# Six clips and the decay and bonus columns of the first recurrence, made on POOL instead of DVE

## The reference, cut to what matters

```python
tf = sigmoid(sum(time_emb, -1))[:, None, None]
decay = exp(-exp(w))[None, :] * (0.5 + 0.5 * tf[:, :, 0])
ek  = exp(minimum(k, 30.0));  ekv = ek * v
# forward and backward scans over time:  a = a*decay + ekv_t ;  b = b*decay + ek_t
euk = exp(minimum(u + k, 30.0))
num = nf + nb - ekv + euk * v
den = df + db - ek + euk
base = sigmoid(r) * (num / maximum(den, 1e-08))
out = base * (0.8 + 0.2 * tf)
```

## Time and profile before

| | before |
|---|---|
| median of 3 runs | 438.07 us |
| the profiled execution | 438.29 us |
| its span, first to last instruction | 436.6 us |
| mean granted TensorE clock | 0.975 |
| busy: PE, DVE, POOL, ACT | 389.6, 327.8, 248.0, 232.9 us |

### The profile page before, as it was taken

One profiled execution on the slowest core, in us unless ns is written; L12 is line 12 of the kernel. 1 busy time (PEld: TensorE's weight loads), 2 busy tenths in 40 slices (PEclk: granted clock), 3 DMA queues, 4 the chain that ended last, 5 costly groups with the idle time before them and its releaser, 6 DMA issues.

```text
span 436.6 us, 6831 instructions
## 1 busy us (share of the span) xinstructions
PE 389.6 (89%) x2025; PEld 244.8 (56%) x2025; DVE 327.8 (75%) x620; ACT 232.9 (53%) x462; POOL 248.0 (57%) x347
## 2 busy tenths in 40 slices
PE   7898999999899999975895899999999999886895
PEld 7676788655455555643685445455445545563463
DVE  5998798999999999979887456654855452068993
ACT  5724594466676766757785423232322323259792
POOL 5475008489678998424840655785687366124641
PEclk9999999999999999999995699999999999999998
DMA  6910003455465644329311277926975710330011
GB/s 205 411 64 0 2 1 148 179 189 171 170 222 198 210 166 162 127 81 368 132 50 48 79 261 244 389 92 233 328 233 192 279 39 14 96 128 0 24 38 36
DMA packets 27347, 65.57 MB, mean 150 GB/s; under 512 B 3360, under 2 KB 7840, under 8 KB 26672
## 3 DMA queue, kind: packets, MB, share of 16 engines
q1 hardware_dynamic: 24320, 58.93, 38.9%
q0 software_dynamic: 1904, 5.18, 3.8%
q10 hardware_dynamic: 1088, 1.05, 0.7%
HBM read 102.83 MB, written 4.78 MB: 247 GB/s over the span
## 4 chain that ended last, share of the span: by engine, by line
PE 52%; DVE 29%; issue 8%; DMA 4%; ACT 4%; POOL 1%; SPq 1%; DVEq 0%; POOLq 0%; ACTq 0%
PE bank L2055 14%; PE bank L2089 8%; PE bank L1822 7%; DVE hx L1341 4%; DVE fw L1130 4%; DVE bw L1133 3%; PE bank L1667 3%; PE bank L1668 3%; PE bank L1669 3%; DVE fw L1138 2%; DMA dn<-in_dn 2%; PE bank L2066 2%; PE bank L1919 2%; DVE xp L1399 2%; PE bank L1744 2%
## 5 line engine op out<-in xcount | busy, mean ns | idle before, releaser
L2055 PE MATMUL bank<-gu,xbT 128*64 128x512 f32 (+1 forms) x320 | 71.3, 583 | 1.2 <-ACT xbT L964 0.9
L1822 PE MATMUL bank<-hx,w2raw 128*128 128x512 f32 x128 | 67.3, 607 | 4.6 <-DVE hx L1341 3.8
L852 ACT ACTIVATE rl<-bank 128x512 f32<-128x512 f32 x64 | 38.1, 595 | 38.3 <-PE bank L1669 37.5
L1562 DVE TENSOR_TENSOR hm<-bank,sl 128x512 f32<-128x512 f32 (+1 forms) x20 | 13.5, 675 | 48.8 <-issue 31.8
L1667 PE MATMUL bank<-xlhi,w1hi 128*128 128x512 f32 x64 | 49.3, 771 | 0.0
L2055 PEld LDWEIGHTS bank<-gu,xbT 128*64 128x64 f32 x320 | 25.9, 137 | 33.8 <-issue 28.8
L1341 DVE TENSOR_TENSOR hx<-bank,cwb 128x512 f32<-128x512 f32 x64 | 42.0, 659 | 3.1 <-ACT bank L856 3.0
L1138 DVE RECIPROCAL fw<-fw 128x256 f32<-128x256 f32 x23 | 39.8, 1730 | 0.0
L2089 PE MATMUL bank<-dn,hT 128*64 128x256 f32 x304 | 37.0, 384 | 2.7 <-ACT hT L976 0.3
L856 ACT ACTIVATE bank<-rl 128x512 f32<-128x512 f32 x64 | 38.1, 597 | 0.0
L634 POOL DMA_INDIRECT y_rows<-yb,dest_i x19 | 21.4, 1126 | 22.8 <-ACT yb L983 21.6
(11 more groups left out here) (312 smaller groups left out, 913.5 us busy)
## 6 DMA issues: line engine op xcount, KB each, us to landing
gu<-in_gu SPq DMA_DIRECT2D x86, 512.0 KB
dn<-in_dn SPq DMA_DIRECT2D x43, 512.0 KB
cwb<-cw_rows SPq DMA_DIRECT2D x32, 512.0 KB, 4.1
traw<-in_t SPq DMA_DIRECT2D x3, 1024.0 KB, 7.4
w1raw<-in_w SPq DMA_DIRECT2D x8, 256.0 KB, 4.7
w2raw<-in_w SPq DMA_DIRECT2D x8, 256.0 KB, 4.3
kT<-in_kt SPq DMA_DIRECT2D x4, 256.0 KB, 5.5
x<-in_x SPq DMA_DIRECT2D x2, 512.0 KB, 7.2
```

Source lines behind the costliest of these rows:

```text
L852: act.activation(rl[:, u % 3, :], bank[u % 4][:], ACT.Relu).then_inc(sem("r_ready"), 1)
L1822: pe.matmul(bank[4 + s][:], w2raw[:, e // 4 % 2, e % 4, :], hx[:, 0, u % 4, :], start=(e == 0), stop=(e == E0 - 1), skip_group_check=True) ...
L2055: ins = pe.matmul(bank[2 * (b % 2) + up][part(g), inner(b)], xbT[:, b % 2, k, part(g)], rhs, start=(k == 0), stop=(k == KC - 1))
```

## The change

Clips of batches 1 to 3 (six instructions) and the columns move from DVE's program to POOL's. On POOL a clip has a second operation, max with 0.0, which changes no value since an exponential is not negative. The `ubk` copy becomes four instructions, one per layer. DVE's first decay product signals `decay_ready`, which POOL waits for ahead of the columns. The semaphore `te_sum` counts the columns' instructions; DVE's `clip_key(0)` and `clip_bonus(0)` stay.

```diff
+            def clip_key(b):
+                pool.wait_ge(sem("ek_raw"), b + 1)
+                pool.tensor_scalar(ekk[:, 2 * b:2 * b + 2, 1, :], ekk[:, 2 * b:2 * b + 2, 1, :], E30, 0.0, ALU.min, ALU.max
+                                   ).then_inc(sem("ek_ready"), 1)
+            def clip_bonus(b):
+                pool.wait_ge(sem("eu_raw"), 2 * b + 2)
+                pool.tensor_scalar(GT[:, 1, 2 * b:2 * b + 2, :], GT[:, 1, 2 * b:2 * b + 2, :], E30, 0.0, ALU.min, ALU.max
+                                   ).then_inc(sem("euk_ready"), 1)
+            def side_columns():
+                per_b = tfb[:].rearrange("p i (o b q) -> p i o b q", o=1, q=1)
+                lbk = [P, 4, B, KC]
+                pool.wait_ge(sem("decay_ready"), 1)
+                pool.tensor_tensor(dec[:], wl[:].rearrange("p l (o k) -> p l o k", o=1).to_broadcast(lbk),
+                                   per_b[:, 2, :, :, :].to_broadcast(lbk), ALU.mult).then_inc(sem("te_sum"), 1)
+                for l in range(4):
+                    pool.tensor_scalar(ubk[:, l, :, :], ul[:, l:l + 1, :].to_broadcast([P, B, KC]), 1.0, 0.0, ALU.mult, ALU.add
+                                       ).then_inc(sem("te_sum"), 1)
+                pool.tensor_scalar(tfb[:, 3, :], tfb[:, 0, :], 0.2, 0.8, ALU.mult, ALU.add).then_inc(sem("te_sum"), 1)
+                pool.tensor_scalar(tfb[:, 1, :], tfb[:, 0, :], -0.2, -0.8, ALU.mult, ALU.add).then_inc(sem("te_sum"), 1)
...
             side_value(0)
+            clip_key(1)
             first_value(0)
             first_value(1)
             side_value(1)
+            clip_bonus(1)
+            side_columns()
+            clip_key(2)
             first_value(2)
+            clip_bonus(2)
             side_value(2)
+            clip_key(3)
             first_value(3)
+            clip_bonus(3)
             split_side(0)
             side_value(3)
             first_value(4)
...
-            pool.wait_ge(sem("te_sum"), 2)
+            pool.wait_ge(sem("te_sum"), 8)
...
-            def side_columns():
-                dve.tensor_tensor(dec[:], wl[:].rearrange("p l (o k) -> p l o k", o=1).to_broadcast(lbk),
-                                  per_b[:, 2, :, :, :].to_broadcast(lbk), ALU.mult)
-                dve.tensor_copy(ubk[:], ul[:].rearrange("p l (o k) -> p l o k", o=1).to_broadcast(lbk)).then_inc(sem("te_sum"), 1)
-                dve.tensor_scalar(tfb[:, 3, :], tfb[:, 0, :], 0.2, 0.8, ALU.mult, ALU.add)
-                chain(dve.tensor_scalar(tfb[:, 1, :], tfb[:, 0, :], -0.2, -0.8, ALU.mult, ALU.add))
...
-            between = {(0, 1): [lambda: clip_bonus(0), side_columns], (0, 3): [lambda: clips(1)],
-                       (1, 3): [lambda: clips(2)], (2, 3): [lambda: clips(3)],
+            between = {(0, 1): [lambda: clip_bonus(0)],
                        (5, 3): [lambda: make_cond(0, 0), lambda: make_cond(0, 1)],
```

More of the change, by code:

```diff
@@ L1082, in clip_bonus @@
                                   ).then_inc(sem("euk_ready"), 1)
-            def clips(b):
-                clip_key(b)
-                clip_bonus(b)
             dve.wait_ge(sem("wl_ready"), 3)
@@ L1091, in _ @@
             chain(dve.tensor_scalar(tfb[:, 2, :], tfb[:, 0, :], 0.5, 0.5, ALU.mult, ALU.add))
-            lbk, per_b = [P, 4, B, KC], tfb[:].rearrange("p i (o b q) -> p i o b q", o=1, q=1)
+            per_b = tfb[:].rearrange("p i (o b q) -> p i o b q", o=1, q=1)
             decf = dec[:].rearrange("p l b k -> p (l b k)")
[L1094 to L1097, removed]
-            def side_columns():
-                dve.tensor_tensor(dec[:], wl[:].rearrange("p l (o k) -> p l o k", o=1).to_broadcast(lbk),
-                                  per_b[:, 2, :, :, :].to_broadcast(lbk), ALU.mult)
-                dve.tensor_copy(ubk[:], ul[:].rearrange("p l (o k) -> p l o k", o=1).to_broadcast(lbk)).then_inc(sem("te_sum"), 1)
-                dve.tensor_scalar(tfb[:, 3, :], tfb[:, 0, :], 0.2, 0.8, ALU.mult, ALU.add)
-                chain(dve.tensor_scalar(tfb[:, 1, :], tfb[:, 0, :], -0.2, -0.8, ALU.mult, ALU.add))
+            dve.tensor_tensor(bank[6][:, 0:NBLK].rearrange("p (b k) -> p b k", k=KC),
+                              wl[:, 0:1, :].to_broadcast([P, B, KC]),
+                              per_b[:, 2, 0, :, :].to_broadcast([P, B, KC]), ALU.mult).then_inc(sem("decay_ready"), 1)
+            dve.wait_ge(sem("decay_ready"), 1)
             def col(ap, i):
```

## The result

The changed kernel takes 433.33 us (median of 7 runs, 432.89 to 434.69), the kernel before 436.6 (7 runs): ratio 0.9923, 95% interval 0.9904 to 0.9942. The same kernel again, in a later comparison: 434.13 against 436.64, ratio 0.9941 (0.9919 to 0.9962). I had forecast 439.4, slightly slower. The chance for what happened, rival 1, was 0.19.

The account below looks back on a forecast made before the run. DVE was taken as saturated up to its gain at 39.90 us; 2.98 us off DVE, less 0.25, plus 4.06 of waits for POOL gave +1.3 us: 439.4 us against a median of 438.07, range 438.1 to 440.3.

Parts of the forecast that it names:

- rival 1: POOL's clips cost 0.62 us, or anything under 1.33; POOL keeps up, DVE saves 2.7 us: 435.4 us; chance 0.19.
- What bounds the stage: From 6.24 to 40.3 us DVE is saturated, while POOL has 12.1 us free.
- the hand-over one to one: A microsecond DVE saves or loses ahead of its gain at 39.90 us shifts everything behind by as much.
- What DVE gives up: Columns and clips of batches 1 to 3, blocks 0 to 2: 2.98 us off DVE, 2.7 us net.
- The 0.25 for PE's warm-up: At DVE's first reciprocal, about 0.25 us of saving lost waiting for PE's first denominator, held by a warm-up assumed fixed.
- the columns' 0.99: DVE's column instructions, from 8.24 us to the next scan at 9.23: 0.99 us saved by moving them.
- the price of a clip: Called c: one min-max clip of 512 elements on POOL, estimated 2.0 us, six clips 12.0 us; bounds 0.62 and 2.29.
- the 4.06 us of waits for POOL: DVE's newton_step of blocks 3 and 4 waits for POOL's first_value, 1.89 and 2.17 us.
- The walk along POOL: POOL's queue added up in order from start-to-start lengths; first_value(4) ends at 31.1 us, leaving DVE 1.3 us late.
- Rival 3: PE idles about 2 us twice at blocks 3 and 4, its clock falls: 443 us; chance 0.04.
- Rival 2: Clips cost 2.29 us or more, or POOL's reads are slowed; between clip_bonus(3) and first_value(4): 441.2 us; chance 0.18.
- Rival 4: PE's adds, not DVE, set the stage's pace, so the change doesn't shorten it: 438 us; chance 0.04.

Follow-up runs that it names:

- The kernel with the prices: The changed kernel plus eleven tensor_scalar instructions in POOL's idle time, to time operation pairs; min-max took 0.61 us, add-min 1.93 us; no median given.
- The kernel with add-min: The changed kernel with POOL's clips written as add 0.0 then min, not min then max: 438.41 us, ratio 1.0039 to the kernel before.

## Why the prediction was wrong, step by step

- What bounds the stage, DVE's saturation and the hand-over one to one: right. The gain came 2.65 us earlier and layer 0's matmuls behind it 2.6.
- What DVE gives up, 2.7 us net: the number is right, partly by luck. Measured at the gain are 2.65, or 2.78 counted from DVE's first clip. Up to the first reciprocal 1.69 us were saved (12.83 to 11.27, and DVE had started 0.13 later), where 1.64 had been added up; the clips of batches 2 and 3 gave 1.09 together and not 1.34. The 0.25 for PE's warm-up did not show: its 36 matmuls took 6.04 us in the profile after and 7.09 before, so PE was ready earlier, and the two errors cancel. That was a length I took for fixed, and in another profile the term is there. The kernel with the prices holds the whole change, its warm-up was long, DVE waited 0.25 us, and its gain came at 37.56:

```profile
3.02 7.18 PE L1743 MATMUL bank<-ident 128*128 128x128 f32 x36 [3.02 <-POOL ident L474]
...
11.54 1.76 DVE L1220 RECIPROCAL fw<-bank 128x256 f32<-128x256 f32 x1 [0.25 <-PE bank L1805]
```

- Part of the columns' 0.99 was no work of theirs: one instruction lasted 0.70 instead of 0.15 beside POOL. Its like falls on another instruction when only one part is moved, so each part alone was worth less.
- **The step that failed is the price of a clip: 2.0 us estimated, 0.62 measured.** I saw that the pair of operations sets the price, and then put min-max into the slow class because L503 "has a minimum in it". The rows had two classes and none of them min-max; a minimum in another pair says nothing of this one. The lower bound, L557, was the truth. With it went the 4.06 us of waits for POOL: DVE had none, and the shift is -2.65 where +1.3 stood.
- The forecast of 439.4 was also counted from 438.07, the median of three runs; seven runs give 436.6. Of the 6.1 us between forecast and measurement 4.0 are the shift, 1.5 are this, and some 0.6 are left. Rival 1's 435.4 lies too high for the same reason, while its mechanism is the one that was found.
- The walk along POOL: right. Given the price of a clip it forecast the end within 0.2 us at c = 2.0 and 1.57 and DVE's waits within 0.3 at c = 2.0. Rival 1 used it too, to say that POOL keeps up.
- The Trainium skill's rule that 1-input work is near line rate on GpSimd (GPSIMD Engine Reference, section When to use GPSIMD) puts add, multiply and max in one row and tells no pairs apart. It holds within half as much again for min-max and multiply-add (0.61 to 0.62 us against an estimated 0.43 from the page) and fails by a factor of 3.5 for min alone and of four to five for add-min, add-add and max-multiply.
- Rival 3, PE's clock during the stage: no fall after the change, but there PE had no long waits either. The kernel with add-min is the test: PE stood idle 2.41 and 2.29 us for POOL, and the granted clock was 1.00 in every window from 15 to 41.4 us. Rival 2 had c of 2.29 or more; max-multiply came nearest, 2.27 from start to start. Rival 4, PE and not DVE sets the pace: out, since the gain came earlier by what DVE gave up.

## What to carry to other kernels

Before work is moved to GpSimd, time the exact pair of operations there: here one pair costs 0.61 us and its neighbour 1.93 for the same function, which is the difference between 0.6% faster and 0.4% slower. Where a bound of an unknown cost lies far from the other and the walk shows from which price on it decides (here 1.78 us), the sign of the forecast is the chance of that price and deserves no more confidence than the row it is taken from. A helper engine's queue can be walked through: start-to-start lengths and its fixed order gave each wait to some tenths. And when two engines read SBUF at once, look at the lengths of their instructions before the rest of a difference is put down to the change: here one meeting was worth 0.6 us, a quarter of the gain.

## What was unexpected in the hardware

- On POOL a minimum with a second, neutral operation (min, then max with 0.0) took 0.61 us at 128x512; the minimum alone took 1.51.
- DVE instructions of 4 to 32 elements took 0.59 to 0.71 us, instead of 0.15 to 0.18, while POOL was reading SBUF; at 163 us one of 128x256 took 1.02 instead of 0.41 when POOL's started in the same hundredth of a microsecond or 0.01 earlier, and POOL's took 0.99 instead of 0.74 when DVE's was 0.01 ahead. So part of an instruction's length in a profile can be its neighbour's.
- PE's warm-up of 36 equal matmuls took between 5.88 and 7.18 us in different executions. The windows show 7 matmuls per microsecond at first and 11 later, from 9 us on in the kernel before (7.09 us) and from 7 us on in the changed one (6.04 us), with the granted clock at 1.00 in all windows read. What sets the moment stays open.
